# One search round of one row tile moved from VectorE to ScalarE, one group ahead, and tiles loaded in the order 2, 1, 0

## The chip, the cores and the metric

The kernel runs on one core of a Trainium2 chip. The metric is the device time of one execution in microseconds (us). Three runs of the kernel before took 4093.86, 4098.3 and 4099.82 us; the median is 4098.3 us. In this document PE is TensorE, DVE is VectorE, ACT is ScalarE, POOL is GpSimd and SP is SyncE, as in the profile.

## The reference, cut to what matters

A graph layer runs two steps (`STEPS = 2`) over 3327 nodes. Each step builds an attention matrix from the features. Of every row only the largest softmax entries are kept, those that together reach the share 0.9 (top-p); what is kept is normalized again and multiplied with the features. After the two steps come a layer norm and a second graph layer (masked attention over the adjacency matrix).

```python
logits = Q @ W2 @ K.T / TAU
idx = jnp.argsort(-logits, axis=1)
vals = jnp.take_along_axis(logits, idx, axis=1)
csum = jnp.cumsum(jax.nn.softmax(vals, axis=1), axis=1)
k_i = jnp.sum(csum < P_NUC, axis=1) + 1        # P_NUC = 0.9
...
masked = jnp.where(keep, logits, -jnp.inf)
A = jax.nn.softmax(masked, axis=1)
...
Xf = Rf @ Xf
Xb = Rb @ Xb
Xa = A @ Xa
Z = Z + (Xf @ U1[s] + Xb @ U2[s] + Xa @ U3[s])
```

## The kernel before

The function `layer_step` is called twice, for step 0 and step 1. The 3327 rows are 26 tiles of 128 rows; three tiles make a group, so that a step has nine groups g = 0 to 8, and the last of them has two tiles. Within a group the tiles have the roles r = 0, 1 and 2. Instead of sorting, the kernel searches in each row for the threshold above which the exponentials add up to 0.9 of the row's total: `BISECT = 19` rounds for each tile.

VectorE searches in the tiles 0 and 1, in turns. A round is one pass over the tile's 3327 columns (`evaluate`, L658, which adds up all entries above the threshold `mid`), then two operations on one column (`judge`, L665, compares the sum with the target; `move`, L670, multiplies the threshold). `move` of one tile stands after `evaluate` of the other. ScalarE searches in tile 2 alone. Its round is two passes (L608, a Sign whose sum counts the entries above the threshold; L613, a Relu whose sum tells how far they lie above it), one small operation in between (`sides`, L474) and four small ones behind (`settle`, L482 to L489), each waiting for the one before it.

A group has 38 beats b, two per round: on VectorE beat 2*it + r is round `it` of tile r, on ScalarE beat 2*it ends after the Sign pass and beat 2*it + 1 after the Relu pass. The work of the other groups is dealt out to these beats, in an order fixed in the code on each engine:

- PE computes the logits of group g + 1 into two PSUM banks (L785, L786), from beat 7 on; VectorE takes them to SBUF (`take`, L637) and finds the row maximum (`highest`, L643).
- ScalarE turns each of the three loaded tiles into exponentials (`exponent`, L464) at beats 20, 29 and 37 of group g, for the tiles of group g + 1 in the order in which they are loaded (`LOADS`).
- PE transposes the cut tiles of group g - 1 (L838), ScalarE copies them out of PSUM (`evacuate`, L497, from beat 1 on, one per beat), and PE multiplies them with the features (`attend`, L849). PE also sweeps the adjacency matrix (L797, L803, L806), which DMAs on SP's queue bring.
- In step 0 the results of group g - 1 are mixed for step 1 from beat 21 on (`columns`, `mixed`, `high_parts` on ScalarE, `low_parts` on VectorE).

At the end of its search VectorE cuts tiles 0 and 1 (`cut`, L678), and it cuts tile 2 in beat 2 of the next group. It starts a group with `begin` for tiles 0 and 1 (L647, L648), which waits for their exponentials. ScalarE starts its own with L469 and L470, after the last exponential and the last `settle` of the group before. The six row buffers are shared by two groups (`home`).

Of the kernel before, what the change touches and what calls it, by code (L numbers as in the profile page):

```python
# [7 lines left out]
ALU = mybir.AluOpType  # L8
ACT = mybir.ActivationFunctionType
# [7 lines left out]
N = 3327  # L17
# [292 lines left out]
def roles(g):  # L310

    return [r for r in (0, 1, 2) if 3 * g + r < NT]


def load_order(g):

    return [r for r in (2, 0, 1) if r in roles(g)]


def home(g, r):  # L320

    return 3 * (g % 2) + (r + g // 2) % 3


def rate(it):
# [7 lines left out]
def layer_step(nc, sem_in, psum, sb_in, s, qk, s_op, a_op, env):  # L333
# [13 lines left out]
    LOADS = [(g, r) for g in range(TRIPLES) for r in load_order(g)]  # L347
# [7 lines left out]
    with ExitStack() as c:  # L355
# [4 lines left out]
        adump = sb(tag + "adump", [P, N], I8 if s else BF16)  # L360
# [5 lines left out]
        nb, Z, target, mid, hit, mass, kept, rk = (  # L366
            sb(tag + n, [P, 6], F32) for n in ("nb", "Z", "target", "mid", "hit", "mass", "kept", "rk"))
# [2 lines left out]
        u12 = sb(tag + "u12", [P, KC, 2 * D], F32)  # L370
        S = {n: sem(tag + n) for n in (
            "lg_done", "lg_free", "nb_ready", "exp_done", "w_ready", "rk_ready", "tr_done", "ev_done", "ax_done",
            "acc_free", "slab_used", "sa_free", "rows_zero", "rates", "a_eval", "a_begun", "a_base", "a_over", "a_sgn", "a_fac", "a_mid",
            "weights")}
        if s == 0:
            strip = sb("strip", [P, 2, 7 * P], F32)
# [83 lines left out]
        def _(act):  # L460
# [12 lines left out]
            def sides(g, n):  # L473
                nc.scalar.activation(base[:], st(mid, g, 2), ACT.Identity, scale=float(N), bias=st(target, g, 2)).then_inc(S["a_base"], 1)  # L474

            def settle(g, it):
                n = BISECT * g + it
# [4 lines left out]
                nc.scalar.activation(over[:], cnt[:], ACT.Identity, scale=st(mid, g, 2), bias=base[:]).then_inc(S["a_over"], 1)  # L482
# [6 lines left out]
                nc.scalar.activation(st(mid, g, 2), st(mid, g, 2), ACT.Copy, scale=fac[:]).then_inc(S["a_mid"], 1)  # L489
# [138 lines left out]
        def _(dve):  # L628
# [15 lines left out]

            def begin(g, r):
                dve.wait_ge(S["exp_done"], LOADS.index((g, r)) + 1)
                nc.vector.tensor_scalar(st(target, g, r), st(Z, g, r), P_NUC, None, ALU.mult).then_inc(begun[r], 1)  # L647
                nc.vector.tensor_scalar(st(mid, g, r), st(Z, g, r), LEAST * 2.0 ** LOG_STEP, None, ALU.mult).then_inc(begun[r], 1)  # L648

            def evaluate(g, it, r):  # L650
                n = BISECT * g + it
                if it == 0:
# [3 lines left out]
                if n + r >= 1:  # L656
                    dve.wait_ge(mass_done[1 - r], n + r)
                nc.vector.scalar_tensor_tensor(out=dump[:], in0=row(g, r), scalar=st(mid, g, r), in1=row(g, r),  # L658
                                               op0=ALU.is_gt, op1=ALU.mult, accum_out=st(mass, g, r)).then_inc(mass_done[r], 1)

            def judge(g, it, r):
                n = BISECT * g + it
                up, down = rate(it)
                dve.wait_ge(mass_done[r], n + 1)
                nc.vector.tensor_scalar(st(hit, g, r), st(mass, g, r), st(target, g, r), up - down, ALU.is_ge, ALU.mult).then_inc(hit_ready[r], 1)  # L665

            def move(g, it, r):
# [59 lines left out]
            for g in range(TRIPLES):  # L727
                for r in range(2):
                    begin(g, r)
                for it in range(BISECT):  # L730
                    for r in range(2):
                        b = 2 * it + r
                        evaluate(g, it, r)
                        if it + r >= 1:
                            move(g, it + r - 1, 1 - r)
                        judge(g, it, r)
                        if g >= 1 and b == 2:
                            cut(g - 1, 2)
                        if g >= 1 and b == 3:
# [654 lines left out]
```

## Time and profile before

| what | value |
|---|---|
| median of three runs | 4098.3 us (4093.86 to 4099.82) |
| the profiled execution's own time | 4103.59 us |
| its span | 4101.8 us |
| DVE busy | 3651.9 us, 89% of the span |
| PE busy | 3071.6 us, 75% |
| ACT busy | 2989.3 us, 73% |
| mean granted TensorE clock | 0.885 of full speed |

The shares are means over the whole span. The two layer steps take it from about 60 us to 3430 us; what follows is the middle phase and the second graph layer, which the diff does not touch. In the page's slices ScalarE is at 9 tenths and more through most of the layer steps, and at 1 or 2 tenths in the last group of each step and in the second layer.

### The profile page before, as it was taken

Reading aid. Unit: us, or ns where it says so; the run is one execution under the profiler, and the core shown is the slowest. Engines: PE = TensorE matmul, PEld = TensorE weight load, DVE = VectorE, ACT = ScalarE, POOL = GpSimd, SP = SyncE. Lnnn points to the kernel's source line nnn. Section 1 sums busy time; section 2 is a strip of 40 time slices with the busy share of each in tenths; the row PEclk is TensorE's granted clock in tenths of the full one; section 3 lists DMA queues with packets and bytes.
Section 4 is the critical chain, followed back from the end, with each engine's and each line's share of the span. In section 5 each row is a group of like instructions: output and inputs, shape, how many; then the busy total and the mean of one; then the engine's idle time right before and its main releaser. Section 6 shows DMA issues by size and latency. Waiting matters only on the chain. (4 is left out here: it accounts for less than half of the span.)

```text
span 4101.8 us, 41817 instructions
## 1 busy us (share of the span) xinstructions
PE 3071.6 (75%) x14330; PEld 2114.4 (52%) x14330; DVE 3651.9 (89%) x4924; ACT 2989.3 (73%) x3969; POOL 360.4 (9%) x430
## 2 busy tenths in 40 slices
PE   5567778787687875288687877968789246988888
PEld 4356656566565664135354443534445244666666
DVE  6999999999999997899999999999989675666666
ACT  6999999999999921799999999999991022222232
POOL 2000000000000000000000000000000063322222
PEclk8689989899898987699898998989899678999999
DMA  2112122221221220311111111111111052122221
GB/s 85 59 51 95 51 70 75 70 83 53 79 75 61 84 69 16 128 55 32 41 43 32 44 34 43 34 39 39 38 45 39 11 176 97 59 82 92 78 78 47
DMA packets 108901, 254.26 MB, mean 62 GB/s; under 512 B 11984, under 2 KB 47888, under 8 KB 105360
## 3 DMA queue, kind: packets, MB, share of 16 engines
q1 hardware_dynamic: 89968, 224.32, 17.0%
q10 hardware_dynamic: 18720, 27.27, 1.8%
q8 instruction: 113, 1.85, 0.2%
q14 instruction: 100, 0.82, 0.1%
HBM read 217.47 MB, written 34.08 MB: 61 GB/s over the span
## 5 line engine op out<-in xcount | busy, mean ns | idle before, releaser
L658 DVE SCALAR_TENSOR_TENSOR s_dump<-s_rows,s_mid 128x3327 bf16<-128x3327 f32 x684 | 2518.2, 3682 | 0.7 <-issue 0.2
L608 ACT ACTIVATE s_adump<-s_rows,s_mid 128x3327 bf16<-128x3327 f32 (+1 forms) x304 | 933.6, 3071 | 9.9
L613 ACT ACTIVATE s_adump<-s_rows,s_mid 128x3327 bf16<-128x3327 f32 (+1 forms) x304 | 930.0, 3059 | 5.6 <-ACT s_xa_out L506 2.8
L806 PE MATMUL bank<-x,s_slab 128*128 128x512 f32 x1352 | 620.3, 612 | 0.0
L849 PE MATMUL bank<-hb,s_wT 128*128 128x256 f32 x1352 | 358.8, 410 | 126.0 <-ACT s_wT L497 126.0
L849 PE MATMUL bank<-xab,s_wT 128*128 128x256 f32 x1352 | 350.5, 404 | 115.7 <-ACT s_wT L497 115.7
L806 PEld LDWEIGHTS bank<-x,s_slab 128*128 128x128 f32 x1352 | 267.4, 198 | 319.4 <-issue 313.3
L1228 ACT ACTIVATE e_wh<-bank 128x512 f16<-128x512 f32 (+1 forms) x182 | 102.4, 565 | 445.8 <-PE bank L1327 445.7
L497 ACT ACTIVATE s_wT<-bank 128x512 f32<-128x512 f32 (+1 forms) x364 | 201.2, 553 | 285.5 <-PE bank L838 285.5
L838 PE MATMUL bank<-ident,s_rows 128*128 128x128 f32 x1352 | 224.6, 292 | 171.6 <-DVE s_rows L678 171.6
L849 PEld LDWEIGHTS bank<-hb,s_wT 128*128 128x128 f32 x1352 | 259.6, 203 | 176.8 <-ACT s_wT L497 82.1
L785 PE MATMUL bank<-kh,qs 128*128 128x512 f16 (+1 forms) x364 | 145.3, 399 | 273.6 <-DVE s_rows L637 263.4
L849 PEld LDWEIGHTS bank<-xab,s_wT 128*128 128x128 f32 x1352 | 257.8, 201 | 167.1 <-ACT s_wT L497 74.2
L806 PE MATMUL bank<-hb,s_slab 128*128 128x257 f32 x1352 | 343.0, 408 | 0.0
L806 PEld LDWEIGHTS bank<-hb,s_slab 128*128 128x128 f32 x1352 | 280.8, 209 | 54.8 <-issue 5.3
L838 PEld LDWEIGHTS bank<-ident,s_rows 128*128 128x128 f32 x1352 | 183.9, 154 | 235.1 <-DVE s_rows L678 179.8
L637 DVE TENSOR_SCALAR_CACHE_REDUCE s_rows<-bank 128x512 f32<-128x512 f32 (+1 forms) x364 | 232.9, 644 | 58.7 <-PE bank L786 56.7
L1208 POOL TENSOR_TENSOR e_rows<-e_rows,e_adj 128x3328 f32<-128x3328 f32 x26 | 187.8, 7225 | 427.6 <-ACT e_rows L1214 427.6
L785 PEld LDWEIGHTS bank<-kh,qs 128*128 128x128 f16 x364 | 38.2, 105 | 344.6 <-DVE s_rows L637 308.9
L1293 DVE TENSOR_TENSOR e_wl<-bank,e_wh 128x512 f16<-128x512 f32 (+1 forms) x182 | 117.8, 650 | 107.9 <-ACT e_wh L1228 107.8
L678 DVE SCALAR_TENSOR_TENSOR s_rows<-s_rows,s_mid 128x3327 f32<-128x3327 f32 x52 | 191.4, 3680 | 0.9
L1338 PE MATMUL bank<-sup,e_wh 128*128 128x256 f16 x676 | 185.3, 274 | 7.4 <-DVE e_wl L1293 7.4
(171 smaller groups left out, 4646.2 us busy)
## 6 DMA issues: line engine op xcount, KB each, us to landing
s_slab<-adjT_dram SPq DMA_DIRECT2D x104, 448.0 KB, 3.9
e_adj<-adjR_dram SPq DMA_DIRECT2D x26, 1664.0 KB, 7.1
s_slab<-adjT_dram SPq DMA_DIRECT2D x104, 384.0 KB, 3.5
strip<-adjR_dram SPq DMA_DIRECT2D x52, 448.0 KB, 3.5
strip<-adjR_dram SPq DMA_DIRECT2D x52, 384.0 KB, 3.3
su_d<-s_su_out ACTq DMA_DIRECT2D x26, 256.0 KB, 2.1
zu_d<-s_zu_out ACTq DMA_DIRECT2D x26, 256.0 KB, 2.0
sx_d<-s_sx_out ACTq DMA_DIRECT2D x26, 256.0 KB, 2.0
```

What stands on the lines that cost most here:

```text
L497: nc.scalar.activation(wT[:, n % 2, 0:w], bank_of("quad", n)[:, 0:w], ACT.Copy).then_inc(S["ev_done"], 1)
L608: nc.scalar.activation(adump[:], row(g, 2), ACT.Sign, bias=st(mid, g, 2), accum_out=cnt[:]).then_inc(S["a_eval"], 1)
L613: nc.scalar.activation(adump[:], row(g, 2), ACT.Relu, bias=st(mid, g, 2), accum_out=gap[:]).then_inc(S["a_eval"], 1)
L637: nc.vector.tensor_scalar(rows[:, home(g, r), ch * CH:ch * CH + w], psL[n % 2][:, 0:w], 1.0, None, ALU.mult, ALU.max, accum_out=mx[:, home ...
L658: nc.vector.scalar_tensor_tensor(out=dump[:], in0=row(g, r), scalar=st(mid, g, r), in1=row(g, r), op0=ALU.is_gt, op1=ALU.mult, accum_out=s ...
L678: nc.vector.scalar_tensor_tensor(out=row(g, r), in0=row(g, r), scalar=st(mid, g, r), in1=row(g, r), op0=ALU.is_gt, op1=ALU.mult, accum_out ...
L785: nc.tensor.matmul(psL[n % 2][:, 0:w], lhs, kh2[:, cols], start=True, stop=False)
L806: ins = nc.tensor.matmul(acc, slab[:, i % NSLAB, j - PIECES[p], :], s_op[:, j, 0:SN], start=False, stop=(j == NT - 1))
L838: ins = nc.tensor.transpose(bank[:, k * P:(k + 1) * P], rows[:, home(g, r), j * P:(j + 1) * P], ident[:])
L849: ins = nc.tensor.matmul(psA[f % 2][:, 0:D], wT[:, n % 2, k * P:(k + 1) * P], a_op[:, j, 0:D], start=(j == 0), stop=(j == NT - 1))
L1208: nc.gpsimd.tensor_tensor(em[:, t % 3], em[:, t % 3], adj[:, t % 3], ALU.mult).then_inc(S["w_ready"], 1)
L1338: nc.tensor.matmul(acc, wh[:, n % 4, blk], sup[:, j, 0:D], start=(j == 0), stop=False)
```

## The change

Of each group g = 1 to 8 (`lent(g)`), round 0 of tile 1 is no longer done by VectorE in group g, but by ScalarE while it still works on group g - 1: right behind its own round 15 (`LENT`, beats 30 and 31). ScalarE does it in its own way (`lend`: a Sign pass, a Relu pass, `sides`, `settle`, and two small operations ahead), with the threshold kept negative as it keeps its own. VectorE's `begin` waits for that round, computes the target as before and turns the sign of the threshold. VectorE's `evaluate` and `judge` of beat 1 are left out in these groups; its `move` for tile 0 stays. For that tile 1 must be there earlier, so the load order is 2, 1, 0 in place of 2, 0, 1: the second exponential, at beat 29, is now that of tile 1, the last, at beat 37, that of tile 0. `home` is rewritten so that the first tile loaded still takes the buffer of tile 0 of two groups before, the second that of tile 1, the third that of tile 2.

```diff
+LENT = 15
...
-    return [r for r in (2, 0, 1) if r in roles(g)]
+    return [r for r in (2, 1, 0) if r in roles(g)]
...
-    return 3 * (g % 2) + (r + g // 2) % 3
+    return 3 * (g % 2) + (2 - r if g // 2 % 2 else r)
...
+def lent(g):
+
+    return 1 <= g < TRIPLES
+
+
+def settled(g, it):
+
+    return BISECT * g + it + sum(lent(h + 1) for h in range(g)) + (1 if lent(g + 1) and it > LENT else 0)
...
+            def lend(g):
+                n = settled(g - 1, LENT) + 1
+                act.wait_ge(S["exp_done"], LOADS.index((g, 1)) + 1)
+                nc.scalar.activation(st(target, g, 1), st(Z, g, 1), ACT.Copy, scale=2.0 * P_NUC).then_inc(S["l_begun"], 1)
+                nc.scalar.activation(st(mid, g, 1), st(Z, g, 1), ACT.Copy, scale=-LEAST * 2.0 ** LOG_STEP).then_inc(S["l_begun"], 1)
+                act.wait_ge(S["l_begun"], 2 * g)
+                nc.scalar.activation(adump[:], row(g, 1), ACT.Sign, bias=st(mid, g, 1), accum_out=cnt[:]).then_inc(S["a_eval"], 1)
+                sides((g, 1))
+                act.wait_ge(S["a_eval"], 2 * n + 1)
+                nc.scalar.activation(adump[:], row(g, 1), ACT.Relu, bias=st(mid, g, 1), accum_out=gap[:]).then_inc(S["a_eval"], 1)
+                settle(n, (g, 1), 0)
...
                     if 2 in roles(g):
-                        settle(g, it)
+                        settle(n, (g, 2), it)
+                        if it == LENT and lent(g + 1):
+                            lend(g + 1)
...
             def begin(g, r):
                 dve.wait_ge(S["exp_done"], LOADS.index((g, r)) + 1)
+                if r == 1 and lent(g):
+                    dve.wait_ge(S["a_mid"], settled(g - 1, LENT) + 2)
                 nc.vector.tensor_scalar(st(target, g, r), st(Z, g, r), P_NUC, None, ALU.mult).then_inc(begun[r], 1)
-                nc.vector.tensor_scalar(st(mid, g, r), st(Z, g, r), LEAST * 2.0 ** LOG_STEP, None, ALU.mult).then_inc(begun[r], 1)
+                if r == 1 and lent(g):
+                    nc.vector.tensor_scalar(st(mid, g, r), st(mid, g, r), -1.0, None, ALU.mult).then_inc(begun[r], 1)
+                else:
+                    nc.vector.tensor_scalar(st(mid, g, r), st(Z, g, r), LEAST * 2.0 ** LOG_STEP, None, ALU.mult).then_inc(begun[r], 1)
...
-                        evaluate(g, it, r)
-                        if it + r >= 1:
-                            move(g, it + r - 1, 1 - r)
-                        judge(g, it, r)
+                        if not (lent(g) and b == 1):
+                            evaluate(g, it, r)
+                            if b >= 1 and not (lent(g) and b == 2):
+                                move(g, it + r - 1, 1 - r)
+                            judge(g, it, r)
+                        else:
+                            move(g, 0, 0)
```

ScalarE's order behind its round 15 of group 1 in step 0. The first rows are the last two of that round (`fac`, `mid`); the row with `s_xT` is `columns` of the third tile. Before:

```order
L487 ACTIVATE s_fac<-s_sgn,s_mean_rate 128x1
L489 ACTIVATE s_mid<-s_mid,s_fac 128x1
L608 ACTIVATE s_adump,s_cnt<-s_rows,s_mid 128x3327
L474 ACTIVATE s_base<-s_mid,s_target 128x1
L529 ACTIVATE s_xT<-bank 128x512
```

Now, with nine more rows between the two rounds:

```order
L497 ACTIVATE s_fac<-s_sgn,s_mean_rate 128x1
L499 ACTIVATE s_mid<-s_mid,s_fac 128x1
L505 ACTIVATE s_target<-s_Z 128x1
L506 ACTIVATE s_mid<-s_Z 128x1
L508 ACTIVATE s_adump,s_cnt<-s_rows,s_mid 128x3327
L485 ACTIVATE s_base<-s_mid,s_target 128x1
L511 ACTIVATE s_adump,s_gap<-s_rows,s_mid 128x3327
L492 ACTIVATE s_over<-s_cnt,s_base,s_mid 128x1
L495 ACTIVATE s_sgn<-s_gap,s_over 128x1
L497 ACTIVATE s_fac<-s_sgn,s_mean_rate 128x1
L499 ACTIVATE s_mid<-s_mid,s_fac 128x1
L630 ACTIVATE s_adump,s_cnt<-s_rows,s_mid 128x3327
```

Nothing is taken from ScalarE's order; its own round 16 now stands behind nine instructions, two of them passes over 3327 columns.

VectorE's order at the start of group 2 in step 0, behind the cut of tile 1. Before:

```order
L647 TENSOR_SCALAR s_target<-s_Z 128x1
L648 TENSOR_SCALAR s_mid<-s_Z 128x1
L647 TENSOR_SCALAR s_target<-s_Z 128x1
L648 TENSOR_SCALAR s_mid<-s_Z 128x1
L658 SCALAR_TENSOR_TENSOR s_dump,s_mass<-s_rows,s_mid 128x3327
L665 TENSOR_SCALAR s_hit<-s_mass,s_target 128x1
L658 SCALAR_TENSOR_TENSOR s_dump,s_mass<-s_rows,s_mid 128x3327
L670 TENSOR_SCALAR s_mid<-s_hit,s_mid 128x1
L665 TENSOR_SCALAR s_hit<-s_mass,s_target 128x1
L658 SCALAR_TENSOR_TENSOR s_dump,s_mass<-s_rows,s_mid 128x3327
```

Now:

```order
L673 TENSOR_SCALAR s_target<-s_Z 128x1
L677 TENSOR_SCALAR s_mid<-s_Z 128x1
L673 TENSOR_SCALAR s_target<-s_Z 128x1
L675 TENSOR_SCALAR s_mid<-s_mid 128x1
L691 SCALAR_TENSOR_TENSOR s_dump,s_mass<-s_rows,s_mid 128x3327
L697 TENSOR_SCALAR s_hit<-s_mass,s_target 128x1
L701 TENSOR_SCALAR s_mid<-s_hit,s_mid 128x1
L691 SCALAR_TENSOR_TENSOR s_dump,s_mass<-s_rows,s_mid 128x3327
```

One pass and one `judge` are gone; `move` of tile 0 now stands directly behind its own `judge` and ahead of its own next pass.

## Rows read from the trace of the kernel before

**Rows 1.** The page: busy us, share of the span, instructions.

```profile
PE 3071.6 (75%) x14330; PEld 2114.4 (52%) x14330; DVE 3651.9 (89%) x4924; ACT 2989.3 (73%) x3969; POOL 360.4 (9%) x430
```

**Rows 2.** Windows view: one group of step 0, one of step 1.

```profile
core 0: us, PE busy (x) PEld busy (x) DVE busy (x) ACT busy (x) POOL busy (x), PEclk, DMA share, GB/s
930.70:1104.20 173.50, 134.87 (x660) 106.07 (x660) 172.32 (x221) 170.28 (x228) 3.46 (x3) 0.90 0.22 71
2376.80:2554.40 177.60, 139.90 (x450) 79.71 (x450) 170.41 (x213) 166.16 (x207) 0.00 (x0) 0.89 0.13 38
```

**Rows 3.** Timeline, ACT starts two successive groups in each step (start, us).

```profile
1102.87 0.20 ACT L469 ACTIVATE s_target<-s_Z 128x1 f32<-128x1 f32 x1
1276.65 0.20 ACT L469 ACTIVATE s_target<-s_Z 128x1 f32<-128x1 f32 x1
...
2374.22 0.20 ACT L469 ACTIVATE s_target<-s_Z 128x1 f32<-128x1 f32 x1
2551.77 0.20 ACT L469 ACTIVATE s_target<-s_Z 128x1 f32<-128x1 f32 x1
```

**Rows 4.** Waits view of 758.2 to 1104.2 us, step 0 (us, times, longest).

```profile
ACT s_wT L497 <- PE bank L838: 1.4, 2, 0.7
```

**Rows 5.** Waits view of 2376 to 2554 us, step 1.

```profile
DVE s_rows L637 <- PE bank L786: 7.1, 2, 3.8
ACT s_wT L497 <- PE bank L838: 6.3, 3, 3.4
```

**Rows 6.** Timeline of step 1: PE waits for ACT, then ACT for PE.

```profile
2456.26 1.99 PE L849 MATMUL bank<-xab,s_wT 128*128 128x256 f32 x8 [1.36 <-ACT s_wT L497]
...
2461.10 6.17 PE L806 MATMUL bank<-x,s_slab 128*128 128x512 f32 x14
2467.11 0.60 PE L838 MATMUL bank<-ident,s_rows 128*128 128x128 f32 x4
...
2467.75 0.60 ACT L497 ACTIVATE s_wT<-bank 128x512 f32<-128x512 f32 x1 [3.37 <-PE bank L838]
```

**Rows 7.** Timeline of ACT at the start of group 2, step 0.

```profile
407.44 0.38 ACT L482 ACTIVATE s_over<-s_cnt,s_base,s_mid 128x1 f32<-128x1 f32 x1
...
408.83 0.20 ACT L469 ACTIVATE s_target<-s_Z 128x1 f32<-128x1 f32 x1
...
409.16 3.07 ACT L608 ACTIVATE s_adump<-s_rows,s_mid 128x3327 bf16<-128x3327 f32 x1
...
412.41 3.06 ACT L613 ACTIVATE s_adump<-s_rows,s_mid 128x3327 bf16<-128x3327 f32 x1
...
415.46 0.57 ACT L497 ACTIVATE s_wT<-bank 128x512 f32<-128x512 f32 x1
```

**Rows 8.** Timeline of DVE at the start of group 2, step 0.

```profile
409.03 0.21 DVE L670 TENSOR_SCALAR s_mid<-s_hit,s_mid 128x1 f32<-128x1 f32 x1
409.27 3.68 DVE L678 SCALAR_TENSOR_TENSOR s_rows<-s_rows,s_mid 128x3327 f32<-128x3327 f32 x1
...
413.13 3.69 DVE L658 SCALAR_TENSOR_TENSOR s_dump<-s_rows,s_mid 128x3327 bf16<-128x3327 f32 x1
...
416.86 0.21 DVE L665 TENSOR_SCALAR s_hit<-s_mass,s_target 128x1 f32<-128x1 f32 x1
...
420.84 3.68 DVE L658 SCALAR_TENSOR_TENSOR s_dump<-s_rows,s_mid 128x3327 bf16<-128x3327 f32 x1
```

**Rows 9.** Timeline: ACT's last exponential of group 8 ends, DVE begins, both steps.

```profile
1445.46 0.19 ACT L464 ACTIVATION_READ_ACCUMULATOR s_rows<-s_rows,s_nb 128x1 f32 x1
...
1450.72 0.15 DVE L647 TENSOR_SCALAR s_target<-s_Z 128x1 f32<-128x1 f32 x1
...
3079.84 0.19 ACT L464 ACTIVATION_READ_ACCUMULATOR s_rows<-s_rows,s_nb 128x1 f32 x1
...
3086.97 0.15 DVE L647 TENSOR_SCALAR s_target<-s_Z 128x1 f32<-128x1 f32 x1
```

**Rows 10.** Timeline of group 1, step 0: PE waits for DVE, ACT for PE.

```profile
301.25 0.61 PE L785 MATMUL bank<-kh,qs 128*128 128x512 f16 x1 [3.55 <-DVE s_rows L637]
...
308.47 0.60 ACT L497 ACTIVATE s_wT<-bank 128x512 f32<-128x512 f32 x1 [3.78 <-PE bank L838]
```

**Rows 11.** Groups view: table loads on ACT; exponentials in the layer steps.

```profile
L258 ACT ACT_TABLE_LOAD x1 | 1.3, 1283 | 0.7 <-PEq L1387 0.7
...
L464 ACT ACTIVATE s_rows<-s_rows,s_nb 128x3327 f32<-128x3327 f32 x52 | 159.0, 3058 | 28.7 <-DVE s_nb L643 28.7
```

More of the change, by code:

```diff
@@ L372, in layer_step @@
             "lg_done", "lg_free", "nb_ready", "exp_done", "w_ready", "rk_ready", "tr_done", "ev_done", "ax_done",
-            "acc_free", "slab_used", "sa_free", "rows_zero", "rates", "a_eval", "a_begun", "a_base", "a_over", "a_sgn", "a_fac", "a_mid",
+            "acc_free", "slab_used", "sa_free", "rows_zero", "rates", "a_eval", "a_begun", "a_base", "a_over", "a_sgn", "a_fac", "a_mid", "l_begun",
             "weights")}
@@ L471, in begin, with sides, settle @@
                 act.wait_ge(S["a_begun"], 2 * (g + 1))
[L473 to L477, printed above, removed]
+            def sides(k):
+                nc.scalar.activation(base[:], st(mid, *k), ACT.Identity, scale=float(N), bias=st(target, *k)).then_inc(S["a_base"], 1)
+            def settle(n, k, it):
                 up, down = rate(it)
@@ L481, in settle @@
                 act.wait_ge(S["a_eval"], 2 * n + 1)
-                nc.scalar.activation(over[:], cnt[:], ACT.Identity, scale=st(mid, g, 2), bias=base[:]).then_inc(S["a_over"], 1)
+                nc.scalar.activation(over[:], cnt[:], ACT.Identity, scale=st(mid, *k), bias=base[:]).then_inc(S["a_over"], 1)
                 act.wait_ge(S["a_over"], n + 1)
@@ L488, in settle @@
                 act.wait_ge(S["a_fac"], n + 1)
-                nc.scalar.activation(st(mid, g, 2), st(mid, g, 2), ACT.Copy, scale=fac[:]).then_inc(S["a_mid"], 1)
+                nc.scalar.activation(st(mid, *k), st(mid, *k), ACT.Copy, scale=fac[:]).then_inc(S["a_mid"], 1)
                 act.wait_ge(S["a_mid"], n + 1)
+            def lend(g):
[9 more added lines that the diff above has]
+                settle(n, (g, 1), 0)
             def evacuate(n):
@@ L605, in _ @@
                 for it in range(BISECT):
-                    n = BISECT * g + it
+                    n = settled(g, it)
                     if 2 in roles(g):
                         nc.scalar.activation(adump[:], row(g, 2), ACT.Sign, bias=st(mid, g, 2), accum_out=cnt[:]).then_inc(S["a_eval"], 1)
-                        sides(g, n)
+                        sides((g, 2))
                     fill(g, 2 * it)
@@ L646, in begin, with turn_of @@
                 dve.wait_ge(S["exp_done"], LOADS.index((g, r)) + 1)
+                if r == 1 and lent(g):
+                    dve.wait_ge(S["a_mid"], settled(g - 1, LENT) + 2)
                 nc.vector.tensor_scalar(st(target, g, r), st(Z, g, r), P_NUC, None, ALU.mult).then_inc(begun[r], 1)
-                nc.vector.tensor_scalar(st(mid, g, r), st(Z, g, r), LEAST * 2.0 ** LOG_STEP, None, ALU.mult).then_inc(begun[r], 1)
+                if r == 1 and lent(g):
+                    nc.vector.tensor_scalar(st(mid, g, r), st(mid, g, r), -1.0, None, ALU.mult).then_inc(begun[r], 1)
+                else:
+                    nc.vector.tensor_scalar(st(mid, g, r), st(Z, g, r), LEAST * 2.0 ** LOG_STEP, None, ALU.mult).then_inc(begun[r], 1)
+            def turn_of(g, it, r):
+                return BISECT * g + it - (sum(lent(h) for h in range(g + 1)) if r == 1 else 0)
             def evaluate(g, it, r):
-                n = BISECT * g + it
-                if it == 0:
+                n = turn_of(g, it, r)
+                if it == lent(g) * r:
                     dve.wait_ge(begun[r], 2 * (g + 1))
@@ L655, in evaluate @@
                     dve.wait_ge(mid_ready[r], n)
-                if n + r >= 1:
-                    dve.wait_ge(mass_done[1 - r], n + r)
+                before = turn_of(g, it, 1 - r) + r
+                if before >= 1 and not (lent(g) and it + r == 1):
+                    dve.wait_ge(mass_done[1 - r], before)
                 nc.vector.scalar_tensor_tensor(out=dump[:], in0=row(g, r), scalar=st(mid, g, r), in1=row(g, r),
@@ L661, in judge @@
             def judge(g, it, r):
-                n = BISECT * g + it
                 up, down = rate(it)
-                dve.wait_ge(mass_done[r], n + 1)
+                dve.wait_ge(mass_done[r], turn_of(g, it, r) + 1)
                 nc.vector.tensor_scalar(st(hit, g, r), st(mass, g, r), st(target, g, r), up - down, ALU.is_ge, ALU.mult).then_inc(hit_ready[r], 1)
             def move(g, it, r):
-                n = BISECT * g + it
-                dve.wait_ge(hit_ready[r], n + 1)
+                dve.wait_ge(hit_ready[r], turn_of(g, it, r) + 1)
                 nc.vector.tensor_scalar(st(mid, g, r), st(hit, g, r), rate(it)[1], st(mid, g, r), ALU.add, ALU.mult).then_inc(mid_ready[r], 1)
@@ L674, in cut @@
                 if r == 2:
-                    dve.wait_ge(S["a_mid"], BISECT * (g + 1))
+                    dve.wait_ge(S["a_mid"], settled(g, BISECT - 1) + 1)
                 else:
-                    dve.wait_ge(mid_ready[r], BISECT * (g + 1))
+                    dve.wait_ge(mid_ready[r], turn_of(g, BISECT, r))
                 nc.vector.scalar_tensor_tensor(out=row(g, r), in0=row(g, r), scalar=st(mid, g, r), in1=row(g, r),
```

## The prediction

> **What bounds the kernel now.** I begin with the page. DVE is busy 89% of the span and ACT 73% [rows 1], which looks as if ScalarE had over a quarter of its time to give. But these are means over stages; ScalarE is nearly idle in the last group of each step and in the second layer. What the change is worth is decided inside the groups, so I read the windows view of one group in the middle of each step next. In step 0 a group takes 173.50 us, DVE is busy for 172.32 us of it and ACT for 170.28 us: 98%. In step 1 it takes 177.60 us, with DVE at 170.41 and ACT at 166.16 us [rows 2]. Here both engines are full.
>
> So the next question is who waits for whom. The timeline gives ACT's period, from one start of a group to the next: 1276.65 - 1102.87 = 173.8 us in step 0 and 2551.77 - 2374.22 = 177.6 us in step 1 [rows 3]. In 346 us of step 0 (two groups) the waits view lists for ACT only 1.4 us for PE [rows 4], nothing for DVE. 173.8 - 170.3 leaves 3.5 us, which are this 0.7 us per group and the short handovers between dependent small operations. So ScalarE runs there as fast as it can. In step 1 ACT waits 6.3 us per group for PE, none for DVE, while DVE waits 7.1 us for PE [rows 5]. Is PE late there because of DVE? The timeline says no: PE itself had just waited 1.36 us for ACT's copy out of PSUM (2456.26), then came matmuls of the sweep in PE's fixed order (6.17 us of L806 among them), and the transposes that ACT wants only behind them; ACT's copy starts at 2467.75 after 3.37 us idle [rows 6]. This is a loop of ACT and PE alone, and DVE is not in it. Hence in both steps ScalarE, in step 1 with PE, sets the pace of the groups 1 to 7, and DVE keeps up or waits. At the start of group 8 ACT's last exponential is still ahead of DVE's begin: it ends at 1445.46 + 0.19 = 1445.65, DVE begins at 1450.72, 5.1 us later; in step 1 3080.03 and 3086.97, 6.9 us [rows 9]. That is all the slack ScalarE has left.
>
> **What the change takes from VectorE.** Before, from the first pass of a group (413.13) to the next pass on the same tile (420.84) it is 7.71 us [rows 8]. After, one pass is missing, but three dependent operations stand in a row: the pass up to its `judge` takes 416.86 - 413.13 = 3.73 us as before, and then `judge` to `move` and `move` to the next pass are each a handover like that of 409.03 to 409.27, 0.24 us [rows 8]; together 4.21 us. DVE saves 3.5 us in each of 8 groups and 2 steps, 56 us in all, if nothing else holds it. The changed `begin` has the same count of small operations, so 0. Its new wait for ScalarE's lent round costs 0 too: `begin` of tile 0, ahead of it, waits for the exponential of beat 37, and the lent round lies before that in ScalarE's own order.
>
> **What it gives to ScalarE.** The nine added instructions all have their like at the start of a group [rows 7]: the two small ones 409.16 - 408.83 = 0.33 us; the Sign pass with `sides` 412.41 - 409.16 = 3.25; the Relu pass 415.46 - 412.41 = 3.05; `settle` 408.83 - 407.44 = 1.39. Sum 8.02 us, in front of round 16, eight times in each step: 64.2 us per step. No DMA is issued by them. What lies behind them in ScalarE's queue is all the rest of the group, above all the last exponential, for which VectorE's `begin` waits, and then the next group's copies out of PSUM, for which PE waits.
>
> A bound from below: could ScalarE absorb it? In step 0 it has 0.7 us per group of waits for PE to give; in step 1 6.3 us. The latter come from the ACT-PE loop, which moves as a whole when ACT is late, so I take 0 and keep 6.3 us per group for the range. From above: the period after can't be much more than ACT's old period plus 8.02 us, unless a new wait arises (last rival).
>
> **Step 0.** ACT ends its last exponential 64.2 us later, less what it waited because DVE was behind and no longer will: in group 1 PE waited 3.55 us for VectorE's take and ACT then 3.78 us for PE [rows 10]; with VectorE relatively earlier this goes, and something like the 0.7 us of the later groups stays. I take 3.1 us off: +61.1 us. DVE's slack of 5.1 us is eaten first, and in group 8 DVE has one pass less, 3.5 us: 61.1 - 5.1 - 3.5 = +52.5 us at the end of the step.
>
> **Step 1.** 64.2 - 6.9 (slack) - 3.5 (group 8) = +53.8 us.
>
> **The order of loads.** Same count of tiles, same beats, the buffer taken is freed by the same tile in the order; `begin` of tile 1 waited, before, for the last exponential just as `begin` of tile 0 does now. 0 us; the cover is that both begins stand together ahead of the first pass.
>
> **Sum.** 4103.59 + 52.5 + 53.8 = 4209.9 us for an execution like the profiled one. That one lies 5.3 us above the median of the runs shown; from the median it is 4098.3 + 106.3 = 4204.6. I predict 4205 us, 2.6% slower. A measurement of this kernel can tell about 0.2% (8 us) from no change.
>
> **A rule that says otherwise.** The Trainium skill, page "Perfetto Trace Analysis", section "Identifying the Most-Contended Engine", says in effect that the engine with the highest occupancy is the one to relieve first; its section "Optimizing Scalar/DVE Operations" adds that moving some to ScalarE may pay when the DVE is saturated. On whole-span shares that is this change. The trace agrees with neither as applied to the span: the windows show ScalarE at 98% and the DVE at 99% of the same group. By the rule the result would be the first rival's.
>
> **Rivals.**
>
> 1. *VectorE is the bound, ScalarE has room* (faster). For it: DVE's 172.3 of 173.5 us and 89% over the span. It would give 4098.3 - 56 = 4042 us. Against: ACT would have to take 8.0 us in a group in which it is idle for 3.5. The point from which it decides: ACT's idle time per group would have to be at least the added work, and not be tied to PE. Chance 5%.
> 2. *Step 1 absorbs what it can.* If the 6.3 us that ACT waits for PE per group shrink as ACT comes later, the lent round costs there 8.02 - 6.3 = 1.7 us in seven groups and 8.0 in the first, 20 us: 20 - 6.9 - 3.5 = +10 us, with step 0 as above +62: 4161 us. For it: the waits are there. Against: PE waited for ACT just before them [rows 6]. Chance 12%, half-way cases included.
> 3. *A new wait behind the lent round* (slower still). In step 0 the lent round stands ahead of `columns` of the third tile; PE's next matmuls need it, the last logits stand behind those in PE's queue, VectorE's last takes behind these, and ACT's last exponential needs them. The nearest row: all waits of an exponential for VectorE come to 28.7 us [rows 11], over seven exponentials, 4.1 us each; in seven groups of step 0 that is 29 us, 4234 us. It decides only if PE and VectorE need more than the five beats, over 20 us, that remain between `columns` at beat 32 and the exponential at beat 37. Chance 8%.
> 4. *No change at all*, were ScalarE's round to fit exactly into the slack: needs 8 us where rows 2 show 3.5. Chance 2%.
> 5. A reload of ScalarE's function tables at each switch between the exponential and the passes: one row, one load for the whole kernel, although 52 exponentials stand between such passes [rows 11]. So 0 us and no chance. By the page "ScalarE: Activation LUTs" of the Trainium skill, section "What ACT_TABLE_LOAD costs", a switch to another set takes about 2.66 us; the row shows that none is made here.
>
> **How the numbers follow.** The forecast has 73%: its own range is 4192 to 4218, from the spread of the runs shown (6 us) and from the terms that I set by judgment (3.1 us, the 0.7 us). For 8 in 10 the range must reach towards rival 2, so 4165 to 4222; outside it lie rival 1, 3 and 4 and part of 2. Faster 5%, the same 2%, slower 93%.
>
> **What would show it.** Right: in the windows of the middle groups DVE falls to about 168.8 us busy in step 0 while the group takes about 181.8 us; ACT's start to start is 181.8 in step 0 and 185.6 in step 1; VectorE's idle time moves to its `begin`, released by ScalarE's exponential, 4 us and more per group, or in step 0 to `low_parts`, which needs ScalarE's `high_parts`, since 16 Sign and 16 Relu passes are added, each of about 3.07 us. The second layer takes the same time. Wrong in the first way: group times of 169 to 174 us. Wrong in the second: ACT's waits for L838 in step 1 fall from 6.3 us to nearly nothing. Wrong in the third: ACT L464 waits for VectorE's `highest` in the middle groups. What would make it wrong altogether is a pace of ScalarE that is itself set by VectorE through a wait that the view does not list.

## The result, and the profile after

The changed kernel takes 4217.24 us (median of four runs, 4215.47 to 4219.64), the kernel before 4099.06 us: ratio 1.0291, 95% interval 1.0274 to 1.0309. It is 118 us slower; 106 us were forecast. The profiled execution after has 4219.64 us and a span of 4217.8 us, 116.0 us more than before.

The changed kernel has other line numbers: `take` is L661, the logits' matmuls L819 and L820, the sweep L840, the transposes L872, `evacuate` L519, `attend` L883, the exponential L475. In the kernels of experiments 5 and 9 the transposes are L877 and `attend` is L888.

The page's busy row of the kernel after, which answers to [rows 1]:

```profile
PE 3080.1 (73%) x14330; PEld 2122.6 (50%) x14330; DVE 3598.2 (85%) x4860; ACT 3114.1 (74%) x4145; POOL 344.3 (8%) x430
```

DVE has 53.7 us less to do and ACT 124.8 us more, and the shares of the span still look as if ScalarE had a quarter to spare. The windows view of one middle group of each step, to be laid beside [rows 2]:

```profile
core 0: us, PE busy (x) PEld busy (x) DVE busy (x) ACT busy (x) POOL busy (x), PEclk, DMA share, GB/s
964.20:1145.10 180.90, 134.41 (x660) 106.28 (x660) 169.00 (x217) 178.24 (x239) 2.13 (x3) 0.90 0.21 68
2648.30:2836.10 187.80, 139.49 (x450) 80.02 (x450) 166.97 (x207) 174.11 (x218) 0.00 (x0) 0.87 0.12 36
```

In step 0 ACT is busy 178.2 of 180.9 us, DVE 169.0: VectorE is idle for 12 us of this group. The timeline, ACT's starts of the groups (against [rows 3]):

```profile
963.37 0.20 ACT L480 ACTIVATE s_target<-s_Z 128x1 f32<-128x1 f32 x1
1144.28 0.20 ACT L480 ACTIVATE s_target<-s_Z 128x1 f32<-128x1 f32 x1
...
2649.59 0.20 ACT L480 ACTIVATE s_target<-s_Z 128x1 f32<-128x1 f32 x1
2837.31 0.20 ACT L480 ACTIVATE s_target<-s_Z 128x1 f32<-128x1 f32 x1
```

ACT's period is 180.9 us in step 0 (173.8 before) and 187.7 us in step 1 (177.6 before). The waits view of 2648 to 2836 us (against [rows 5]) has, besides ACT's waits on its own small operations:

```profile
DVE s_rows L661 <- PE bank L820: 16.5, 3, 8.2
...
ACT s_wT L519 <- PE bank L872: 8.4, 4, 3.4
DVE s_target L673 <- ACT s_rows L475: 4.0, 1, 4.0
```

VectorE waits 20.5 us in this group, 16.5 of them for PE's logits and 4.0 for ScalarE's last exponential. ScalarE's own waits for PE are 8.4 us where they were 6.3. The begins of group 8 (against [rows 9]):

```profile
1501.58 0.19 ACT L475 ACTIVATION_READ_ACCUMULATOR s_rows<-s_rows,s_nb 128x1 f32 x1
...
1503.87 0.15 DVE L673 TENSOR_SCALAR s_target<-s_Z 128x1 f32<-128x1 f32 x1
...
3207.94 0.19 ACT L475 ACTIVATION_READ_ACCUMULATOR s_rows<-s_rows,s_nb 128x1 f32 x1
...
3208.16 0.15 DVE L673 TENSOR_SCALAR s_target<-s_Z 128x1 f32<-128x1 f32 x1 [1.02 <-ACT s_rows L475]
```

VectorE begins the last group of step 0 at 1503.87 instead of 1450.72, 53.2 us later, and that of step 1 at 3208.16 instead of 3086.97, 121.2 us later. Its last group then is 3.5 us shorter in each step.

**Where step 1 lost more than the added work.** 187.7 - 177.6 = 10.1 us per group, and the lent round is 8.0 us. The missing 2.1 us are ScalarE's waits for PE. PE's timeline about 40 us into the group, after:

```profile
2692.09 2.67 PE L883 MATMUL bank<-xab,s_wT 128*128 128x256 f32 x8 [2.21 <-ACT s_wT L519]
2694.55 0.63 PE L819 MATMUL bank<-kh,qs 128*128 128x512 f16 x1
2694.98 0.63 PE L820 MATMUL bank<-kl,qs 128*128 128x512 f16 x1
2695.41 6.78 PE L840 MATMUL bank<-x,s_slab 128*128 128x512 f32 x14
2702.03 0.60 PE L872 MATMUL bank<-ident,s_rows 128*128 128x128 f32 x4
```

and the same instructions in the kernel before:

```profile
2416.26 1.97 PE L849 MATMUL bank<-xab,s_wT 128*128 128x256 f32 x8 [2.21 <-ACT s_wT L497]
2418.06 0.38 PE L785 MATMUL bank<-kh,qs 128*128 128x512 f16 x1
2418.28 0.38 PE L786 MATMUL bank<-kl,qs 128*128 128x512 f16 x1
2418.50 6.17 PE L806 MATMUL bank<-x,s_slab 128*128 128x512 f32 x14
2424.50 0.60 PE L838 MATMUL bank<-ident,s_rows 128*128 128x128 f32 x4
```

From the start of the first to the start of the transposes it is 9.94 us after and 8.24 us before, for the same work in the same order. The matmuls themselves take longer (2.67 us for `attend` instead of 1.97, 6.78 for the sweep's 14 instead of 6.17), and the granted clock differs. The windows view of 9 us around them, after:

```profile
2691.00:2700.00 9.00, 7.91 (x20) 4.46 (x21) 4.26 (x5) 8.41 (x13) 0.00 (x0) 0.81 0.04 15
```

and before:

```profile
2415.60:2424.60 9.00, 8.34 (x25) 4.53 (x26) 8.42 (x11) 8.41 (x11) 0.00 (x0) 1.00 0.04 15
```

A mean of 0.81 means that TensorE ran for a part of these 9 us at its lower level, 1.2 GHz instead of 2.4 GHz. ScalarE, whose next copy needs those transposes, waits 1.6 us that it did not wait before; another of its waits in the group, 16 us earlier, grew from 2.7 to 3.2 us. Whether the clock is the cause was a question for experiments 5, 6 and 9.

### The profile page after: what moved, and what is told of

Its sections match the earlier page's. It is cut to its first block and busy times, and to the rows that moved or that the text cites. A ratio compares the mean times of both kernels' runs of the same rounds, so it can differ in the third digit from the quotient of the medians.

```text
span 4217.8 us, 41963 instructions
## 1 busy us (share of the span) xinstructions
PE 3080.1 (73%) x14330; PEld 2122.6 (50%) x14330; DVE 3598.2 (85%) x4860; ACT 3114.1 (74%) x4145; POOL 344.3 (8%) x430
## 3 DMA queue, kind: packets, MB, share of 16 engines
q1 hardware_dynamic: 89968, 224.32, 16.5%
## 5 line engine op out<-in xcount | busy, mean ns | idle before, releaser
L691 DVE SCALAR_TENSOR_TENSOR s_dump<-s_rows,s_mid 128x3327 bf16<-128x3327 f32 x668 | 2459.1, 3681 | 1.8 <-issue 0.7
L840 PE MATMUL bank<-x,s_slab 128*128 128x512 f32 x1352 | 617.2, 610 | 0.0
L883 PE MATMUL bank<-xab,s_wT 128*128 128x256 f32 x1352 | 359.0, 411 | 171.7 <-ACT s_wT L519 171.7
L883 PE MATMUL bank<-hb,s_wT 128*128 128x256 f32 x1352 | 354.9, 406 | 149.2 <-ACT s_wT L519 149.2
L840 PEld LDWEIGHTS bank<-x,s_slab 128*128 128x128 f32 x1352 | 267.0, 198 | 316.4 <-issue 310.4
L519 ACT ACTIVATE s_wT<-bank 128x512 f32<-128x512 f32 (+1 forms) x364 | 200.6, 552 | 282.5 <-PE bank L872 282.5
L661 DVE TENSOR_SCALAR_CACHE_REDUCE s_rows<-bank 128x512 f32<-128x512 f32 (+1 forms) x364 | 233.1, 645 | 196.3 <-PE bank L820 194.4
L883 PEld LDWEIGHTS bank<-xab,s_wT 128*128 128x128 f32 x1352 | 261.1, 204 | 224.7 <-issue 122.4
L883 PEld LDWEIGHTS bank<-hb,s_wT 128*128 128x128 f32 x1352 | 257.0, 201 | 201.2 <-ACT s_wT L519 96.4
L819 PE MATMUL bank<-kh,qs 128*128 128x512 f16 (+1 forms) x364 | 147.9, 406 | 278.4 <-DVE s_rows L661 268.1
L840 PE MATMUL bank<-hb,s_slab 128*128 128x257 f32 x1352 | 349.1, 414 | 0.0
L872 PE MATMUL bank<-ident,s_rows 128*128 128x128 f32 x1352 | 231.5, 299 | 156.8 <-DVE s_rows L709 156.8
L840 PEld LDWEIGHTS bank<-hb,s_slab 128*128 128x128 f32 x1352 | 285.0, 212 | 57.5 <-issue 6.2
L872 PEld LDWEIGHTS bank<-ident,s_rows 128*128 128x128 f32 x1352 | 188.7, 157 | 221.3 <-DVE s_rows L709 165.0
L819 PEld LDWEIGHTS bank<-kh,qs 128*128 128x128 f16 x364 | 39.1, 108 | 348.8 <-DVE s_rows L661 312.9
L1372 PE MATMUL bank<-sup,e_wh 128*128 128x256 f16 x676 | 185.6, 274 | 7.4 <-DVE e_wl L1327 7.4
```

The costliest lines, as they stand in the source:

```text
L519: nc.scalar.activation(wT[:, n % 2, 0:w], bank_of("quad", n)[:, 0:w], ACT.Copy).then_inc(S["ev_done"], 1)
L661: nc.vector.tensor_scalar(rows[:, home(g, r), ch * CH:ch * CH + w], psL[n % 2][:, 0:w], 1.0, None, ALU.mult, ALU.max, accum_out=mx[:, home ...
L819: nc.tensor.matmul(psL[n % 2][:, 0:w], lhs, kh2[:, cols], start=True, stop=False)
L840: ins = nc.tensor.matmul(acc, slab[:, i % NSLAB, j - PIECES[p], :], s_op[:, j, 0:SN], start=False, stop=(j == NT - 1))
L872: ins = nc.tensor.transpose(bank[:, k * P:(k + 1) * P], rows[:, home(g, r), j * P:(j + 1) * P], ident[:])
L883: ins = nc.tensor.matmul(psA[f % 2][:, 0:D], wT[:, n % 2, k * P:(k + 1) * P], a_op[:, j, 0:D], start=(j == 0), stop=(j == NT - 1))
```

## The experiments

Each is compared with the kernel before on the same chip. Ratios have the 95% interval in brackets. The diffs are cut to what matters; those of experiments 1, 4, 6, 7 and 10 are against the kernel before, those of 2, 3, 5, 8 and 9 against the changed kernel.

### 1. The load order alone

```diff
-    return [r for r in (2, 0, 1) if r in roles(g)]
+    return [r for r in (2, 1, 0) if r in roles(g)]
...
-    return 3 * (g % 2) + (r + g // 2) % 3
+    return 3 * (g % 2) + (2 - r if g // 2 % 2 else r)
```

Expected: 

> The load order 2, 1, 0 and the new assignment of buffers alone, on the kernel before, without the lent round. My theory: 0, so 4099 us, within 8 us. Rival (part of the loss of 118 us comes from the order or the buffers): over 4107 us.

Measured: 4100.7 us, ratio 1.0002 [0.9992, 1.0011]. The order and the buffers cost nothing; the loss is the lent round's.

### 2. ScalarE's added work without VectorE's relief

```diff
             def lend(g):
-                nc.scalar.activation(st(mid, g, 1), st(Z, g, 1), ACT.Copy, scale=-LEAST * 2.0 ** LOG_STEP).then_inc(S["l_begun"], 1)
+                nc.scalar.activation(hit[:, 2:3], st(Z, g, 1), ACT.Copy, scale=-LEAST * 2.0 ** LOG_STEP).then_inc(S["l_begun"], 1)
...
         def _(dve):
+            lent = lambda g: False
```

The lent round's threshold and target go to columns that nobody else reads.

Expected: 

> The changed kernel, but VectorE does round 0 of tile 1 too; ScalarE's lent round is done in full and its result is not used. My theory (ScalarE sets the pace of groups 1 to 7, VectorE's relief is worth only its last group of each step): 4217 + 2 x 3.5 = 4224 us, 4212 to 4232. Rival (VectorE's relief gives back 3.5 us in each of 16 groups and hides part of ScalarE's cost): 4217 + 56 = 4273 us.

Measured: 4223.7 us, ratio 1.0294 [1.0275, 1.0312], against 1.0291 with the relief. The windows view of the same two groups:

```profile
966.80:1147.80 181.00, 135.93 (x660) 105.90 (x660) 172.59 (x221) 178.33 (x239) 2.12 (x3) 0.88 0.21 68
2467.40:2655.10 187.70, 139.46 (x450) 80.03 (x450) 170.50 (x212) 174.02 (x218) 0.00 (x0) 0.87 0.12 36
```

VectorE is busy 3.5 us more per group than in the changed kernel, and the groups take the same 181.0 and 187.7 us. All of the price is ScalarE's; the rival, at 4273 us, is out.

### 3. VectorE's relief without ScalarE's work

This is the changed kernel without `lend`: nobody does round 0 of tile 1 in groups 1 to 8, and that tile's search starts at a lower threshold.

```diff
                     if 2 in roles(g):
                         settle(n, (g, 2), it)
-                        if it == LENT and lent(g + 1):
-                            lend(g + 1)
...
+                    nc.vector.tensor_scalar(st(mid, g, r), st(Z, g, r), LEAST * 2.0 ** (LOG_STEP / 2 if r == 1 and lent(g) else LOG_STEP), None, ALU.mult).then_inc(begun[r], 1)
```

Expected: 

> The relief alone: VectorE leaves out round 0 of tile 1 in groups 1 to 8 and nobody does it (that tile's search starts at a lower threshold), ScalarE is as before. My theory: ScalarE and PE still set the pace; what can be gained is the slack before group 8 (5.1 and 6.9 us) and the shorter group 8 (2 x 3.5 us), at most 19 us: 4080 to 4090 us. Rival (VectorE is the bound): 4099 - 56 = 4043 us.

Measured: 4090.0 us, ratio 0.9972 [0.9962, 0.9983]. Of the 56 us taken from VectorE some 10 us reach the end. The waits view of 2372 to 2549 us shows where the rest went:

```profile
DVE s_rows L659 <- PE bank L814: 10.5, 3, 4.0
ACT s_wT L519 <- PE bank L866: 6.3, 3, 3.4
```

VectorE waits 10.5 us for PE in place of 7.1 [rows 5]: the 3.5 us saved are waited. Even free of charge the relief would have been worth 0.3%. The forecast for this run was 4080 to 4090 us, so it came out at the upper end.

This run holds something more. ScalarE and PE have here the same work as in the kernel before, and yet group 1 of step 1 takes 179.8 us (ScalarE's start to start, 1834.47 to 2014.25), while groups 2 to 6 take 177.5 to 177.8. The waits view of group 1 (1834.4 to 2014.2 us) has

```profile
ACT s_wT L519 <- PE bank L866: 8.4, 4, 3.4
```

and that of group 2 (2014.2 to 2191.8 us)

```profile
ACT s_wT L519 <- PE bank L866: 6.3, 3, 3.4
```

The windows view of 9 us, from 42 us into either group on:

```profile
1876.50:1885.50 9.00, 8.49 (x21) 4.61 (x22) 9.00 (x11) 8.41 (x10) 0.00 (x0) 0.81 0.04 15
2056.20:2065.20 9.00, 8.91 (x30) 5.07 (x31) 4.55 (x6) 8.41 (x12) 0.00 (x0) 1.00 0.04 15
```

The 2.1 us of waiting and the 0.81 of the changed kernel are both there, without any added work on ScalarE.

### 4. ScalarE with one round less in step 1

This kernel leaves out round 15 of tile 2 in step 1.

```diff
-                    if 2 in roles(g):
+                    own = 2 in roles(g) and not (s == 1 and it == 15)
+                    if own:
                         nc.scalar.activation(adump[:], row(g, 2), ACT.Sign, bias=st(mid, g, 2), accum_out=cnt[:]).then_inc(S["a_eval"], 1)
```

Expected: 

> The kernel before, but in step 1 ScalarE leaves out round 15 of its own tile 2 (nobody does it), 7.7 us less for ScalarE in each group; VectorE and PE do all their work. My theory (ScalarE is in the loop that sets step 1's 177.6 us): the group falls to VectorE's 170.4 us, seven times, so 4099 - 7 x 6.3 = 4055 us, 4045 to 4065. Rival (step 1 is bound by PE's work, or by VectorE waiting for PE): 4095 to 4099 us.

Measured: 4065.6 us, ratio 0.9913 [0.9898, 0.9928], 35 us faster where 44 were expected, and just outside the expected 4045 to 4065 us. Two successive groups in the windows view:

```profile
2364.20:2535.20 171.00, 139.27 (x452) 79.53 (x451) 170.25 (x213) 158.69 (x198) 0.00 (x0) 0.91 0.14 40
2535.20:2708.40 173.20, 136.40 (x451) 78.56 (x450) 170.20 (x211) 158.71 (x198) 0.00 (x0) 0.92 0.13 39
```

So ScalarE was in the loop that bound step 1: with less work for ScalarE and none less for PE or VectorE the group falls from 177.6 us to VectorE's 170.3 and a little more. The first of these groups is at that limit; the second takes 2.2 us more though it has the same instructions. In it, and not in the first, ScalarE waits for PE a fifth time, and again the clock differs. The windows view about 40 to 51 us into either group:

```profile
2394.00:2405.00 11.00, 8.79 (x30) 4.93 (x29) 11.00 (x13) 10.41 (x13) 0.00 (x0) 1.00 0.03 12
2565.00:2576.00 11.00, 8.79 (x28) 5.17 (x27) 11.00 (x13) 10.41 (x13) 0.00 (x0) 0.84 0.05 19
```

and in the timeline ACT's copies behind it:

```profile
2405.91 0.60 ACT L500 ACTIVATE s_wT<-bank 128x512 f32<-128x512 f32 x1
...
2579.15 0.60 ACT L500 ACTIVATE s_wT<-bank 128x512 f32<-128x512 f32 x1 [1.61 <-PE bank L842]
```

### 5 and 6. PE kept busy at the start of the group

In step 1, 8 and 14 matmuls of no use stand where PE was idle for 8.3 and 14.5 us: before the first transposes of a group and between them and the first `attend`. Experiment 5 is the changed kernel with them, experiment 6 the kernel before.

```diff
+            def keep_busy(g, n):
+                pe.wait_ge(S["lg_free"], NCH * (3 * g + len(roles(g))))
+                for _ in range(n):
+                    nc.tensor.matmul(psL[0][:, 0:D], ident[:], u12[:, 0, 0:D], start=True, stop=True, skip_group_check=True)
...
+                        if s == 1 and g < TRIPLES and b == 0:
+                            keep_busy(g, 8)
                         for n in due(b, 0, quads, quads):
                             transposes(first + n)
+                        if s == 1 and g < TRIPLES and b == 1:
+                            keep_busy(g, 14)
```

Expected: 

> The changed kernel; in step 1 PE does 8 and 14 matmuls of no use (into a free logits bank) at the two places at a group's start where it was idle for 8.3 and 14.5 us. My theory: the 2.1 us that a group of step 1 costs more than the added 8.0 us come from PE's granted clock, which is at its lower level for 27 us there and again for 3.4 us at the point where ScalarE waits; kept busy, PE stays at the upper level and ScalarE's new wait of 1.6 us goes: 4217 - 7 x 2.1 = 4202 us, 4198 to 4207. Rival (the new wait comes from the order in which VectorE and PE now meet, not from the clock): 4217 us or more.

> The same matmuls of no use in the kernel before, as a control. There the 1.6 us wait doesn't occur, so by my theory 0: 4096 to 4101 us. Rival (the matmuls help or hurt by themselves): outside of that.

Measured: 4219.9 us, ratio 1.0292 [1.0278, 1.0306] for the changed kernel, so no gain, and 4105.5 us, 1.0013 [1.0004, 1.0022], for the control. Both forecasts missed. The control is 5 us slower: in its profiled execution group 1 of step 1 takes 180.7 us instead of 177.5, with 9.3 us of ScalarE's waits for PE, and groups 2 to 6 take 177.5 to 177.8 as before. The miss of experiment 5 tells something: the mean granted clock of a step 1 group rose from 0.87 to 0.90, in the windows view of the changed kernel with them:

```profile
2652.10:2839.80 187.70, 150.48 (x495) 89.47 (x495) 166.94 (x206) 174.02 (x218) 0.00 (x0) 0.90 0.12 36
```

But the waits view of the same group still has ScalarE's 8.4 us:

```profile
ACT s_wT L519 <- PE bank L877: 8.4, 4, 3.4
```

The matmuls did not fill the two long pauses, which are still 4.8 and 6.9 us long, so this run alone does not clear them of the spell 43 us into the group. Experiment 9 does: it leaves them at 9.1 and 14.5 us, and the spell is gone. What remained to be tried were the short pauses of PE just before the spell.

### 9. PE kept busy in its short pauses

```diff
                         for n in due(b, 0, quads, quads):
                             transposes(first + n)
+                        if s == 1 and g < TRIPLES and b in (3, 4, 8):
+                            keep_busy(g, {3: 3, 4: 3, 8: 4}[b])
```

Expected: 

> The changed kernel; in step 1 PE does 3, 3 and 4 matmuls of no use at beats 3, 4 and 8 of each group, where it was idle for 1.9, 2.7 and 2.2 us waiting for ScalarE, the last of them just ahead of the spell of 3.4 us at the lower clock, 43 us after ScalarE's start of the group. My theory (the wait of 1.6 us comes with that spell): if PE's small pauses call up the spell it goes, and with it 2.1 us per group: 4202 us, 4198 to 4208. If spell and wait both stay, it is open what calls up the spell, 4217 to 4222 us. Rival (the wait isn't the clock's doing): the spell goes and the wait stays.

Measured: 4203.9 us, ratio 1.0251 [1.0237, 1.0265], against 1.0291 for the changed kernel: ten matmuls of no use in each group of step 1 take 13 us away by the medians, 16 by the ratios. PE's timeline at the same point:

```profile
2687.62 1.97 PE L888 MATMUL bank<-xab,s_wT 128*128 128x256 f32 x8 [0.48 <-ACT s_wT L519]
2689.43 0.38 PE L819 MATMUL bank<-kh,qs 128*128 128x512 f16 x1
```

The windows view of 9 us around it:

```profile
2687.00:2696.00 9.00, 8.52 (x27) 4.57 (x27) 4.55 (x6) 8.41 (x10) 0.00 (x0) 1.00 0.04 15
```

The waits view of the group, 2644 to 2830 us:

```profile
ACT s_wT L519 <- PE bank L877: 6.3, 3, 3.4
```

PE's pause is 0.48 us instead of 2.21, the clock is at its upper level, `attend` takes 1.97 us as before the change, and ScalarE's waits are back at 6.3 us. Its starts of the groups lie at

```profile
2645.58 0.20 ACT L480 ACTIVATE s_target<-s_Z 128x1 f32<-128x1 f32 x1
2831.16 0.20 ACT L480 ACTIVATE s_target<-s_Z 128x1 f32<-128x1 f32 x1
```

185.6 us apart: 177.6 of before and the 8.0 us of the lent round, to the tenth.

### 7, 8 and 10. The sweep in smaller parts

If ScalarE waits for PE in step 1 because 6 to 9 us of sweep stand ahead of the transposes [rows 6], smaller parts must help, and more than any relief of VectorE. Experiment 7 deals each piece of the sweep out in two halves, experiment 10 in three parts; experiment 8 is the changed kernel with halves. The total work is the same.

```diff
-            def sweep(i):
+            def sweep(i, h):
                 t, p = divmod(i, NPIECE)
+                cutoff = (PIECES[p] + PIECES[p + 1]) // 2
...
-                for j in range(PIECES[p], PIECES[p + 1]):
+                for j in range(*((PIECES[p], cutoff) if h == 0 else (cutoff, PIECES[p + 1]))):
...
-                        for i in due(b, first, BEATS - 1, NPIECE * len(roles(g))):
-                            sweep(3 * NPIECE * g + i)
+                        for i in due(b, first, BEATS - 1, 2 * NPIECE * len(roles(g))):
+                            sweep(3 * NPIECE * g + i // 2, i % 2)
```

Expected: 

> The kernel before, with each piece of PE's sweep cut into two halves at different beats, so that the transposes that ScalarE wants stand behind 3 to 6 us of sweep instead of 6 to 9 us. My theory: ScalarE's waits for PE in step 1 (6.3 us per group) go, and the group falls to ScalarE's own 171.3 us or VectorE's 170.4 us: 4100 - 7 x 6.3 = 4056 us, 4050 to 4070. Rival (PE's total work, or VectorE, holds the group whatever the pieces are): 4095 to 4100 us.

> The changed kernel with the same halved sweeps. My theory: ScalarE's waits for PE, 8.4 us per group of step 1, go, ScalarE's added 8.0 us stay: 4217 - 7 x 8.4 = 4158 us, 4152 to 4175, some 100 us above the kernel with halved sweeps alone. Rival (with the loop with PE eased, ScalarE has room for the lent round): less than 60 us above it.

> The kernel before, with each piece of the sweep in three parts instead of two. My theory (what is left of ScalarE's waits for PE in step 1, 2.5 us per group with halves, still comes from sweep work ahead of the transposes): 4072 - 7 x 2.5 = 4055 us, 4050 to 4066. Rival (what is left comes from something else, or VectorE's 170.4 us and its own waits hold the group): 4068 to 4073 us.

Measured: halves 4071.9 us, ratio 0.9931 [0.9918, 0.9945]; the changed kernel with halves 4182.8 us, 1.0199 [1.0184, 1.0215]; thirds 4048.4 us, 0.9875 [0.9862, 0.9888]. The waits of a middle group of step 1, for halves (2362 to 2536 us) and halves with the lent round (2444 to 2625 us):

```profile
DVE s_rows L637 <- PE bank L786: 3.2, 3, 1.7
ACT s_wT L497 <- PE bank L842: 2.5, 2, 1.3
```

```profile
DVE s_rows L661 <- PE bank L820: 9.8, 5, 5.0
DVE s_target L673 <- ACT s_rows L475: 4.3, 1, 4.3
ACT s_wT L519 <- PE bank L876: 2.5, 2, 1.3
```

Halves leave 2.5 us of the 6.3 in this group and 3.8 to 4.5 in three others, more than I had assumed, hence 4072 and not 4056. With thirds the waits view of a middle group lists no wait of ScalarE or VectorE for PE, and the windows view has

```profile
2353.50:2523.70 170.20, 136.80 (x450) 77.92 (x450) 170.13 (x213) 165.05 (x207) 0.00 (x0) 0.90 0.13 40
```

170.2 us, all of it VectorE's. This is the fastest version measured, 1.25% below the kernel before and a little below the expected 4050 to 4066 us. Not all of it comes from step 1: ScalarE starts step 1 at 1671.7 us with halves and at 1669.9 with thirds instead of 1676.7, 5 and 7 us of the 28 and 52. With halves the lent round costs 111 us on top, more than the 102 expected, and 4182.8 us is outside the expected 4152 to 4175: a middle group goes from 173.6 to 181.6 us, by the lent round's full length.

## Why the prediction was right, point by point

4217 us lies in the forecast's own range of 4192 to 4218, at its very end, and the term of step 1 is what put it there.

- **What bounds the kernel.** ScalarE, in step 1 with PE, sets the pace of groups 1 to 7. Shown by experiments 2 (VectorE's work added back, same group times), 3 (VectorE's work taken away, 10 of 56 us arrive) and 4 (ScalarE's work taken away in step 1, 35 us arrive); PE's part in it by 7 and 10 (PE's order changed, 28 and 52 us arrive). In step 0 of the kernel before the two engines are nearly level: VectorE is busy for 172.3 of 173.5 us [rows 2].
- **The saving on VectorE**, 3.5 us per group. Measured: busy time of a group 172.3 to 169.0 us in step 0, 170.4 to 167.0 us in step 1 (3.3 and 3.4). It went into waits, as forecast, but mostly into others than those named: from the begin of group 1 to that of group 8 of step 0 VectorE waits 75.5 us for PE's logits, 6.8 in `low_parts` and never at `begin`; over the same groups of step 1 116.3 us for the logits and 25.3 at `begin`.
- **The cost on ScalarE**, 8.0 us. Busy time 170.3 to 178.2 and 166.2 to 174.1 us, 8.0 in either; 8.0 us in experiment 9's period.
- **Step 0**, +52.5 us at its end. Measured 53.2 at the begin of group 8 and 3.5 less at its end, 49.7. ScalarE starts step 1 49.5 us later. That this is so near 52.5 is in part luck, for two errors of opposite sign stand in it. ScalarE's last exponential ends 56.1 us later (1501.77 and 1445.65), not 61.1: from group 4 on its period rose by 7.1 us, not 8.0, since its 0.7 us of waits for PE went, and in group 1 those waits fell from 5.0 to 0.7 us, where I had taken 3.1 off. Against that VectorE begins group 8 2.1 us behind that exponential (1503.87 and 1501.58 + 0.19), which I had set to 0: `low_parts` waits for ScalarE and two cuts stand behind it.
- **Step 1**, +53.8 us. This is the mis-sized term. VectorE begins group 8 121.2 us late, 49.7 of it inherited: 71.5, less 3.5 for the shorter group 8, is 68.0, 14 us more than forecast. Seven groups at 2.1 us are 14.7. The step that failed is that of "the ACT-PE loop, which moves as a whole when ACT is late": its order did, its speed did not, and I had taken 0 for it where 2.1 us per group were measured; the start-to-start time forecast for step 1 was 185.6 us and is 187.7. After the change TensorE has a spell at its lower clock at a place of the group where ScalarE waits for the result. Experiment 9 takes spell and wait away together, and in experiments 3 and 4 groups with both and groups with neither stand side by side in one run.
- **The load order**, 0. Experiment 1: 1.0002.
- **Rivals.** The first (VectorE is the bound) is excluded by experiments 2 and 3. The second (step 1 absorbs 6.3 us) had the wrong sign: the waits grew. The third (a new wait behind the lent round in step 0) did not occur; in two groups, 783 to 1145 us, VectorE waits 20.8 us for PE and 2.2 us for ScalarE's `high_parts`, but no exponential of theirs waits for VectorE. The fourth (no change) is excluded by the result, the fifth by the profile after, which has one load of function tables as before.
- **The sum.** 106 forecast, 118 measured; the two steps' terms were off by -3 and +14 us.

What stays open: why PE's clock falls just there. It is no property of the changed kernel, since group 1 of experiment 3 and of experiment 6 has the spell too. PE's pause ahead of that point is 2.1 to 2.2 us with and without it. What goes with it in the traces is an earlier spell: in groups 1 to 7 of step 1 of both kernels and of experiments 1 to 6 and 9 (63 groups) the spell at 43 us is there exactly where TensorE is at its lower level 24.6 us into the group; where it is not there, the earlier spell, if any, is over before 22 us (it lies at 17 to 21 us in the kernel before and at 23 to 27 in the changed one). PE's short pauses between 7 and 25 us differ with it. Which of them leads to the other is not shown, and experiment 9, which added matmuls in three pauses at once and removed both spells, does not tell it.

## What to carry to other kernels

Before work is moved from the engine with the largest busy share to one with a smaller share, read both shares in the stage where the work will land. ACT's 73% of the span was 98% of a group of step 0 and 94% of one of step 1, and most of its idle microseconds there belonged to a loop with PE. What sets the pace is the engine, or the loop of engines, that doesn't wait for the rest, whatever its share; here that was seen from the absence of waits of ACT for DVE, and the cheap cure was an order of PE's work that no longer made ScalarE wait (1.25% faster), not a transfer of work.

## What was not expected of the hardware

TensorE's granted clock fell from its upper to its lower level for a few microseconds about 43 us into groups 1 to 7 of step 1 after the change (mean 0.81 over 9 us against 1.00 before), with no pause of PE over 2.7 us in the 30 us ahead of it, and it cost 2.1 us in each of seven groups. Ten small matmuls of no use per group, in three pauses, kept it up there and made the changed kernel 0.3 to 0.4% faster; 22 of them in the two long pauses at the group's start raised the group's mean clock from 0.87 to 0.90 and gained nothing. What counted here is the clock in the stretch for which another engine waits, not its mean. A group with such a spell can stand beside groups without one in the same run (179.8 and 177.6 us in experiment 3), so a small difference between two kernels may be this and not the edit. The Trainium skill, page "TensorE: Matmul & The Clock Gate", section "Part 1: The HAM clock gate (the "warmup" mystery)", puts the time lost while the clock is still low at the start of matmul work under 1% of a typical kernel's span. That is another stretch than the one measured here: these spells lie in the middle of the kernel, and no run here measures the first stretch alone. Their cost was 14.7 us of 4217, 0.3%.
